# Order of work in the norms, in one masked attention and ahead of an expert layer, in an eight-stage kernel on one core

## The reference

```
_layernorm(x) = (x - mean(x)) / sqrt(var(x) + 1e-5)
x = x + L0_xattn(_layernorm(x), ctx, ...)   # depool: a decayed scan over scaled patches
x = x + L0_ffn(_layernorm(x), ...)          # attention with register rows
x = x + L1_xattn(_layernorm(x), ctx, ...)   # attention over the context and x, 16 heads
x = x + L1_ffn(_layernorm(x), ...)          # 8 experts, top 2 of them per token
x = x + L2_xattn(_layernorm(x), ctx, ...)   # 16 heads, null key; its output has a layer norm
x = x + L2_ffn(_layernorm(x), ...)          # three products with weights +1 and -1
x = x + L3_xattn(ctx, _layernorm(x), ...)   # masked attention, 8 heads of 32
x = x + L3_ffn(_layernorm(x), ...)          # attention over positions, then 8 experts, top 1
```

## Time and profile before

| | |
|---|---|
| median of 3 runs | 2327.0 us (2325.74 to 2328.5) |
| profiled execution | 2322.93 us, of which the span is 2320.9 us |
| granted PE clock, mean over the span | 0.965 |
| PE busy | 2055.2 us, 89% of the span |
| DVE busy | 1259.7 us, 54% |
| ACT busy | 1015.9 us, 44% |
| POOL busy | 303.6 us, 13% |
| transfers | 112.65 MB, mean 49 GB/s |

### The profile page before, as it was taken

How to read it: one execution, slowest core, us unless ns; L and a number is a source line. 1 busy time by engine, 2 the same in 40 slices (tenths; PEclk the granted TensorE clock), 3 DMA queues, 4 the chain that set the end, 5 groups by cost and what they waited for, 6 DMA issues and landing times. The chain is left out here.

```text
span 2320.9 us, 38299 instructions
## 1 busy us (share of the span) xinstructions
PE 2055.2 (89%) x14645; PEld 1546.2 (67%) x14645; DVE 1259.7 (54%) x2526; ACT 1015.9 (44%) x2849; POOL 303.6 (13%) x399
## 2 busy tenths in 40 slices
PE   6789997899988779979999999978998899797796
PEld 4556666566665569856667667656887677575685
DVE  6457775788886234456544454565543555455213
ACT  3247774777775235424333333343321445334122
POOL 0101110222211424300000000012002000000222
PEclk8989999999999989989999999999999999999898
DMA  3000001121221732250000000000001100003452
GB/s 133 19 1 1 1 1 39 32 58 37 54 42 58 258 89 89 84 177 10 10 10 1 10 10 1 1 9 25 1 1 62 37 28 1 22 1 109 150 186 82
DMA packets 88322, 112.65 MB, mean 49 GB/s; under 512 B 18024, under 2 KB 71280, under 8 KB 87248
## 3 DMA queue, kind: packets, MB, share of 16 engines
q1 hardware_dynamic: 83200, 96.63, 13.6%
q0 software_dynamic: 4944, 13.58, 1.7%
HBM read 79.88 MB, written 22.96 MB: 44 GB/s over the span
## 5 line engine op out<-in xcount | busy, mean ns | idle before, releaser
L975 ACT ACTIVATE ca_prob<-bank,ca_nmax 128x512 f32<-128x512 f32 x256 | 174.0, 690 | 73.6 <-DVE ca_nmax L1042 73.6
L1042 DVE TENSOR_REDUCE ca_nmax<-bank 128x1 f32<-128x512 f32 x256 | 164.1, 683 | 41.0 <-PE bank L824 41.0
L975 ACT ACTIVATE na_prob<-bank,na_nmax 128x257 f32<-128x257 f32 x256 | 118.0, 474 | 148.0 <-DVE na_nmax L1042 148.0
L838 PE MATMUL bank<-cst,ca_prob 128*128 128x128 f32 x1024 | 141.5, 280 | 7.6 <-DVE ca_pT L1048 5.9
L838 PEld LDWEIGHTS bank<-cst,ca_prob 128*128 128x128 f32 x1024 | 111.8, 142 | 53.8 <-issue 45.7
L975 ACT ACTIVATE ra_prob<-bank,ra_nmax 128x256 f32<-128x256 f32 x256 | 118.2, 484 | 53.4 <-DVE ra_nmax L1042 53.4
L1042 DVE TENSOR_REDUCE na_nmax<-bank 128x1 f32<-128x257 f32 x256 | 90.9, 417 | 68.7 <-PE bank L824 68.7
L2292 PE MATMUL bank<-sf_h,sf_W 128*128 128x512 f32 x512 | 120.1, 395 | 0.0
L2292 PEld LDWEIGHTS bank<-sf_h,sf_W 128*128 128x128 f32 x512 | 96.0, 188 | 23.5
L2160 PE MATMUL bank<-na_Wkv,na_cxT 128*128 128x512 f32 x224 | 103.6, 605 | 0.0
L1042 DVE TENSOR_REDUCE ra_nmax<-bank 128x2 f32<-128x512 f32 x128 | 82.0, 683 | 39.4 <-PE bank L824 39.4
(11 more groups left out here) (489 smaller groups left out, 4636.3 us busy)
## 6 DMA issues: line engine op xcount, KB each, us to landing
xl_w<-in_L_ffn_w SPq DMA_DIRECT2D x16, 1024.0 KB, 7.7
rf_sent<-rf_w SPq DMA_DIRECT2D x13, 390.0 KB, 5.8
rf_xin<-rf_sent SPq DMA_DIRECT2D x39, 128.0 KB, 2.1
dp_cx<-in_ctx_tok SPq DMA_DIRECT2D x4, 1024.0 KB, 14.6
ca_v<-in_ctx_values SPq DMA_DIRECT2D x8, 512.0 KB, 4.6
rf_W<-in_L_ffn_w SPq DMA_DIRECT2D x8, 512.0 KB, 11.3
rf_rows<-rf_back SPq DMA_DIRECT2D x8, 512.0 KB, 5.4
na_Wkv<-in_L_xattn_Wkv SPq DMA_DIRECT2D x1, 4096.0 KB
```

The source lines that it names most:

```text
L838: mm = pe.transpose(TB[f % 2][:, j * P:(j + 1) * P], prob[:, n % 2, u, c0:c0 + P], ident)
L975: e = act.activation(prob[:, n % 2, u, hh * keys:(hh + 1) * keys], S[u][:, hh * keys:(hh + 1) * keys], ACT.Exp, bias=nmax[:, n % 2, u, hh: ...
L1042: v.tensor_reduce(nmax[:, n % 2, u], S[u][:, 0:W].rearrange("p (h k) -> p h k", h=per), AX.X, ALU.max, negate=True).then_inc(maxed, 1)
```

## The change

Four edits, shown whole below. In the norm's PE list V(gi + 1) is written ahead of SI(gi) instead of behind it, for all groups. In its ACT list the root of the last group follows the root of the one before at once, ahead of `aside(2)` and `affine(1)`, and the table load moves ahead of `affine(NG - 2)`. In its DVE list the last two reciprocals stand in a row ahead of the last two scales. In masked attention the two seats of odd rounds are swapped: values of the next sequence behind the scores, `spread` in the middle. In the expert layer the zeros go out during npa in place of expert 1's weights, which are now loaded when expert 0's rows have arrived.

```diff
@@ layer_norm_phase, tensor
+            variances(0)
             for gi in range(NG):
-                variances(gi)
                 if gi + 2 < NG:
                     spread_mean(gi + 2)
                 if early is not None:
                     early(pe, gi, scaled, rooted, centred, shifted)
+                if gi + 1 < NG:
+                    variances(gi + 1)
                 spread_inverse(gi)
@@ layer_norm_phase, scalar
             for gi in range(NG):
                 if gi + 1 < NG:
                     square(gi + 1)
-                root(gi)
+                if gi + 1 < NG:
+                    root(gi)
+                if gi == NG - 2:
+                    root(NG - 1)
                 if aside is not None:
                     aside(act, gi)
+                if table is not None and gi == NG - 1:
+                    act.wait_ge(table_set, 1)
+                    act.activation(g.hold[:], eps[:], table).then_inc(table_set, 1)
                 if gain is not None and gi >= 1:
                     affine(gi - 1)
-            if table is not None:
-                act.wait_ge(table_set, 1)
-                act.activation(g.hold[:], eps[:], table).then_inc(table_set, 1)
@@ layer_norm_phase, vector
-            for gi in range(NG):
+            for gi in range(NG - 2):
                 invert(gi)
-                if gi + 2 < NG:
-                    centre(gi + 2)
+                centre(gi + 2)
                 scale(gi)
+            invert(NG - 2)
+            invert(NG - 1)
+            scale(NG - 2)
+            scale(NG - 1)
@@ masked_attention_layer
                          late=(2,), place=[[[("front", 1)], [("project",)], [("front", 0)]],
-                                           [[("spread",)], [("front", 2)], []]])
+                                           [[("front", 2)], [("spread",)], []]])
@@ expert_layer, prefetch (runs during npa)
                 load_weights(sp, 0)
-                load_weights(sp, 1)
+                sp.wait_ge(zeroed, 1)
+                for n in range(T // (4 * P)):
+                    sp.dma_start(back[1 + n * 4 * P:1 + (n + 1) * 4 * P, :].rearrange("(t p) d -> p t d", p=P),
+                                 zero[:, :, 0:D]).then_inc(emptied, 16)
@@ expert_layer, sync
-                    for n in range(T // (4 * P)):
-                        sp.dma_start(back[1 + n * 4 * P:1 + (n + 1) * 4 * P, :].rearrange("(t p) d -> p t d", p=P),
-                                     zero[:, :, 0:D]).then_inc(emptied, 16)
                     sp.wait_ge(gate_made, 1)
                     for n in range(T // (4 * P)):
                         sp.wait_ge(row_copied, 2 * n + 2)
                         sp.dma_start(sent[n * 4 * P:(n + 1) * 4 * P, :].rearrange("(t p) d -> p t d", p=P),
                                      rows[:, 4 * n:4 * n + 4]).then_inc(stored, 16)
+                    sp.wait_ge(ldx[0], 32)
+                    load_weights(sp, 1)
                     for e in range(E - 2):
```

## The result

The changed kernel takes 2306.25 us (median of 4 runs, 2300.53 to 2306.87), the kernel before 2326.37 beside it: a ratio of 0.9898, with a 95% interval from 0.9881 to 0.9915. The two medians alone give 0.9914, which is 20.1 us; the ratio on record gives 23.7. Run once more, beside 11 runs of the kernel before, its ratio was 0.9900, [0.9881, 0.9918]. One of those six executions took 5177.94 us and counts in no ratio or median here. Faster by one per cent, and the forecast of 2305.7 held. The profiled execution after took 2305.75 us, with a span of 2303.7 against 2320.9. That is 17.2 us and not the 21.3 of my sum, so part of the agreement of the totals is luck.

A forecast was written before the change was run, and what follows sets the result against it. PE, busy 89% of the span, was taken to bound most of the kernel, leaving waits to win: 14.9 + 3.0 + 3.4 = 21.3 us off 2322.9 gives 2301.6, with the median 4.1 above, 2305.7; range 2300.5 to 2312.

The forecast's parts named there:

- The plain norm: End of n0x, n0f, n2f, n3f: last two reciprocals follow without a wait, last scale 2.2 us earlier each; n1f 1.95.
- Rival (a): Norms: reciprocals in a row but not early, last root late or scale 2 delayed; 14.9 falls to 10, 2310.5; chance 0.12.
- npa: Position norm, ended by ACT: the last affine starts 1.4 us sooner, counting the table load by its row at 1.28 us.
- nax and nxl: Residual norms: POOL's end stays; nax wins 1.35 us, nxl 0, at most 0.9.
- n1x, n2x, n3x: Norms with other ends: one V leaves PE's path, 0.6 us each in n1x and n3x, 0.2 in n2x, held by a transfer.
- Masked attention: 4.2 us of waits for POOL and 1.2 ahead of the keys go, 2.6 lost: 2.8, say 3.0 us; bounds -5 and 5.7.
- the first round: Masked attention's round without value sum and spread: 4.7 us of work against four PE turns of 0.5, 2.6 us lost once.
- The tail: End of masked attention, last spreads behind the value sums: within 0.3 us of even.
- Ahead of the experts: Expert layer: row stores find the transfer queue empty, POOL's gathers start 3.5 us sooner, at most 4.0; 3.4 us taken.
- the landing of the last store: Ahead of the experts: last row store issued 3.0 us behind the first, lands 5.2 later, at 2152.9.
- expert 1 is not late: Expert layer: expert 1's later-issued weights are there by about 2168, product starts at 2177, 9 us left.
- The sum: Whole kernel: norms 14.9, masked attention 3.0 and expert layer 3.4 add to 21.3 us.

The follow-up runs named there:

- transfers: Kernel before with only the transfer order ahead of the last expert layer changed (only zeros in npa, expert 1's weights behind the stores): ratio 0.9983, 3.9 us.
- norms: Kernel before with only the norm edits (orders on PE, ACT and DVE, table load between two affines): ratio 0.9929, 16.5 us gained.
- norms_no_row: Kernel before with the norm edits on PE and ACT, but DVE's old order: ratio 1.0038 to the kernel before, 8.8 us slower.
- mended: Changed kernel, with DVE taking POOL's last add in nax and nxl, old seats in masked attention's first and last such rounds, null attention's small transfers first: 0.9893 to kernel before.
- seats: Kernel before with only the two seats in masked attention exchanged: ratio 0.9988 [0.9976, 1.0001], 2.8 us.
- the three parts alone: norms, seats and transfers, each measured alone against the kernel before: together 23.2 us.
- kv_late: mended with null attention's 4 MB of key and value weights loaded last, on their own semaphore: ratio 0.9879 to the kernel before.
- warm_small: mended with 16 idle PE products (48 in residual norms) over four bank quarters behind a norm's last spread, where no next-block products stand: 0.9858 to kernel before.

## Why the prediction was right

- **The plain norm, 2.2 us:** right to two tenths in n0x, n0f, n1f and n3f, and by its mechanism: reciprocals 0.87 apart, last scale 1.13 behind the one before, V(3) out of the way. Rival (a) feared that the last root would be late by a step. It wasn't, but with nothing to spare: the prediction writes 0.1 us of slack beside 97.36 against 97.37, which is 0.01, and in the trace the second reciprocal starts 0.03 us behind the root's end, as every reciprocal does that a root releases. That the sum of measured steps came out on the right side of so thin a margin is in part luck. The two half edits show that both lists are needed: without DVE's row the plain norm n0f loses 0.9 us, without PE's order it wins 0.1. n2f gave 1.6, because its mean spreads ran at half the clock behind nax (3.79 us for what took 2.81).
- **npa, 1.4 us:** ACT's timeline after, beside the earlier trace rows:

```profile
2118.02 1.51 ACT L300 ACTIVATE XN<-ln_cent,pa_shift,pa_gain 128x512 f32<-128x512 f32 x2
...
2119.54 1.28 ACT L326 ACT_TABLE_LOAD   x1
...
2120.94 2.91 ACT L300 ACTIVATE XN<-ln_cent,pa_shift,pa_gain 128x512 f32<-128x512 f32 x4
```

  The load and the small activation cost 1.40 us between two affines (2119.54 to 2120.94), as the row before said. The 2.66 us of the Trainium skill ("ScalarE: Activation LUTs", What ACT_TABLE_LOAD costs) are not borne out here. The trace gives 3.0, but 1.3 of it is not the edit: in the trace of before the granted clock was 0.80 from 2118 to 2124 us, in the norm's first part, and after 1.00. Against `transfers`, which has the old norm without that, it is 1.7; each step of `affine` and that of the load took about 0.1 less than I had put it.
- **nax and nxl:** mis-sized. "POOL has 0.90 us of idle there to take it up, so its end stays" was true before and false after: POOL's last add itself grew from 2.50 to 2.93, and DVE's from 1.42 to 3.24, since the edit brought DVE's last adds beside POOL's. 0.4 and -0.5 instead of 1.35 and 0. The prediction asked where POOL stood idle, and not which instructions the edit would bring side by side.
- **n1x, n2x, n3x:** one V off PE's path was right in n1x (0.7). n3x gave 0.2, but the traces with the old norm differ there by as much as the term is worth (20.3 to 20.9 us). n2x won 0.35 at the product's start and then lost 1.6, as PE had the lower clock. Why is open: the half clock is there behind 2.49 us of idle PE (2.46 in norms, 2.56 in norms_no_row) and is not behind 2.81 in the second trace of the same kernel or 2.90 in mended, so a longer idle stretch is not what decides it.
- **Masked attention, 3.0 us:** 2.7. Period shorter by 1.05, the first round 2.1 late (I had 2.6). The tail, taken as even, lost 0.4. Mended, the attention gives 5.9 in all. The first round is the least certain of these: from the first maximum to the first output copy the old seats took 34.6 to 36.5 us in six traces, the new ones 37.9 to 38.2 in four.
- **Ahead of the experts, 3.4 us:** 2.4. The step that was off is the landing of the last store: I took the zeros' 5.2 us, a median, and it was 7.24 (6.2 is the median of the four). The other way, it was issued 2.05 us behind the first and not 3.0. Alone the gather stood 8.85 us behind the first store, in the changed kernel 9.36; I had 8.3. The rows do come sooner without the zeros, but two thirds of it in another way than I said: before, the last store was issued 3.71 us behind the first and landed 8.02 later, so 1.66 of the 2.44 us come from the closer issues and 0.8 from the landing. With the zeros ahead the four issues took as long in norms and in seats too (3.74 and 3.63), without them 2.0 to 2.1 in every trace; what slows them is not shown. That expert 1 is not late was right, and so were the 9 us left.
- **The sum:** 19.6 us by the terms' own places in the two traces, against 21.3. The first pair of traces has 2.5 us less: the clock gave 2.4 in two layers and took 1.6 in null attention, and the routed layer with the stall and the rest took 3.2. In the first pair the 1.3 of clock in npa also hides what nax, nxl and the experts fell short. The second comparison has 23 us, as the three parts alone have. Executions of the kernel before alone differ by 13 us (2315.0 to 2328.4 in the first 29).

## What to carry to other kernels

When a chain goes around several engines, an early step is worth nothing until its consumer's list has it early as well: here PE's reordering (with ACT's) without DVE's cost 9 us, DVE's (with ACT's) without PE's some 3, and all three won 16.5. Before moving work off a gap, ask what that work did for the neighbours: V(3) kept PE busy between two spreads, and POOL's add was free only while DVE was elsewhere. With totals this noisy, read each term at its own place in the trace, and have a second trace of each kernel before giving a cause to a microsecond.

## What the runs showed of the hardware

- Products to one 32-partition quarter of a bank took 0.11 us for each record of the profile (10.67 us for 96, which are 48 products); the same shape spread over four quarters 0.034 (1.08 us for 32, 16 products).
- DVE's two adds from SBUF to SBUF took 3.24 us beside POOL's and 1.41 alone, POOL's 2.93 and 2.51.
- A load of the activation table took 1.28 us between two instructions of ACT that followed at once, 1.40 with the small activation that carries it (2119.54 to 2120.94 in the kernel after).
- Behind n0f, where PE is idle for about 2 us and granted 1.00, 3 to 10 us at 1.2 GHz followed in most traces, also while PE was fully busy (the windows of mended above). It was not so in kv_late, with the same idle stretch, nor in the three traces with idle products in it. Summed over windows of 2 us, PE's busy time by the part of the clock not granted, it loses 50 us in the kernel before, 48 after, 44 in its second trace, 43 in mended and 37 in warm_small: executions of one kernel differ by 4.
- ACT stood still for 22 to 25 us in front of a copy whose product was done, in the routed layer, in 4 executions of 14 (24.0 us in the kernel after).
